# Audio tower on one core: W2 loaded and split in quarters, slot indices in one step on VectorE, waits and tables moved on ScalarE, new call orders in opening and ending

## The reference, cut to what matters

```python
# 1. tokens are merged: an MLP gives each token a length, the row is warped to 375 tokens
h = gelu(x @ W1 + b1)                       # 128 -> 512
h = gelu(h @ W2 + b2)                       # 512 -> 512
lens = sigmoid((h @ W3 + b3)[..., 0])
lens = lens / sum(lens) * 375
cs = cumsum(lens); h = warp(x, cs)          # piecewise linear weights, a matmul
# 2. linear attention with 8 memory keys, 8 heads of 64, residual
xn = rmsnorm(layernorm(h)); q, k, v = split(xn @ w_qkv)
context = softmax_over_tokens(k) @ v
h = h + rmsnorm((softmax(q) @ context) @ w_out + b_out)
# 3. switch layer, 16 experts, capacity 225 over all 8 * 375 tokens
xf = layernorm(h); probs = softmax(xf @ switch_w.T + switch_b)
routes = argmax(probs); pos = running count of the route; keep = pos < capacity
y = expert_w[routes] @ xf + expert_b[routes]
out = h + where(keep, y, xf) * max(probs)
```

## Time and profile before

| | us |
|---|---|
| median of 3 runs (lowest, highest) | 397.02 (396.35, 398.41) |
| profiled execution: its time | 397.55 |
| profiled execution: span | 395.8 |
| PE busy | 374.6 (95% of the span) |
| DVE busy | 331.1 (84%) |
| ACT busy | 227.5 (57%) |
| POOL busy | 142.0 (36%) |

### The profile page before, as it was taken

One profiled execution on the slowest core, in us unless ns is written; L12 is line 12 of the kernel. 1 busy time (PEld: TensorE's weight loads), 2 busy tenths in 40 slices (PEclk: granted clock), 3 DMA queues, 4 the chain that ended last, 5 costly groups with the idle time before them and its releaser, 6 DMA issues. The chain is left out here.

```text
span 395.8 us, 7949 instructions
## 1 busy us (share of the span) xinstructions
PE 374.6 (95%) x2706; PEld 326.0 (82%) x2706; DVE 331.1 (84%) x897; ACT 227.5 (57%) x432; POOL 142.0 (36%) x191
## 2 busy tenths in 40 slices
PE   7889989999999999999999999999999989999992
PEld 7667868898888889888888888888888778998892
DVE  3587759969897998889898989798998974988896
ACT  4633448915992499339943895279637743683200
POOL 6101110122168215831484038413840611106880
PEclk9999999999999999999999999999999999999998
DMA  7796002100200030002000200100000052241135
GB/s 220 192 228 235 2 1 55 30 2 3 84 2 20 3 84 2 21 1 84 2 18 5 84 2 11 58 1 1 17 7 0 9 144 69 70 131 31 40 83 127
DMA packets 16358, 21.58 MB, mean 55 GB/s; under 512 B 4882, under 2 KB 11880, under 8 KB 15886
## 3 DMA queue, kind: packets, MB, share of 16 engines
q1 hardware_dynamic: 12350, 18.30, 16.6%
q0 software_dynamic: 2880, 2.35, 2.5%
q10 hardware_dynamic: 1088, 0.42, 0.4%
HBM read 14.40 MB, written 6.62 MB: 53 GB/s over the span
## 5 line engine op out<-in xcount | busy, mean ns | idle before, releaser
L1081 PE MATMUL psB<-W2h,h1l 128*125 128x512 f32 x192 | 77.9, 406 | 2.0 <-DVE h2b L1623 1.3
L1082 PE MATMUL psB<-W2l,h1h 128*125 128x512 f32 x192 | 75.6, 394 | 0.0
L1083 PE MATMUL psB<-W2h,h1h 128*125 128x512 f32 x192 | 75.6, 394 | 0.0
L681 ACT ACTIVATE h2b<-h2b 125x512 f32<-125x512 f32 x48 | 30.1, 628 | 32.9 <-DVE h2b L1623 32.5
L1081 PEld LDWEIGHTS psB<-W2h,h1l 128*125 128x125 f32 x192 | 35.6, 185 | 9.9 <-issue 1.8
L1083 PEld LDWEIGHTS psB<-W2h,h1h 128*125 128x125 f32 x192 | 35.6, 185 | 8.9
L1082 PEld LDWEIGHTS psB<-W2l,h1h 128*125 128x125 f32 x192 | 35.7, 186 | 7.2
L670 ACT ACTIVATE h<-psA,b1c 128x376 f32<-128x376 f32 x64 | 35.4, 579 | 8.4 <-PE psA L1052 8.1
L1623 DVE TENSOR_TENSOR h2b<-psB,b2r 125x512 f32<-125x512 f32 x48 | 32.8, 686 | 8.0 <-PE psB L1083 7.8
L596 POOL DMA_INDIRECT slot_x<-xf,idx_s x18 | 32.5, 1807 | 7.8 <-issue 7.8
L1630 DVE CUSTOM_DVE_ANT_0 h2b<-h2b,W3r 125x512 f32<-125x512 f32 x48 | 32.9, 691 | 1.7 <-ACT h2b L681 1.4
(11 more groups left out here) (266 smaller groups left out, 967.8 us busy)
## 6 DMA issues: line engine op xcount, KB each, us to landing
xTf<-in_x_t SPq DMA_DIRECT2D x16, 187.5 KB, 2.6
xt<-in_x SPq DMA_DIRECT2D x8, 336.0 KB
slot_x<-eb_parts SPq DMA_DIRECT2D x2, 960.0 KB, 13.5
basef<-in_L_tok_W SPq DMA_DIRECT2D x1, 1024.0 KB, 6.9
ewT<-in_expert_t SPq DMA_DIRECT2D x1, 1024.0 KB, 9.3
ewf<-slot_x SPq DMA_DIRECT2D x2, 480.0 KB, 6.1
h2b<-slot_x SPq DMA_DIRECT2D x2, 480.0 KB, 8.5
slot_y<-h SPq DMA_DIRECT2D x4, 240.0 KB, 2.5
```

Of the source, the lines that this page charges most:

```text
L681: nc.scalar.activation(slot, slot, ACT.Gelu).then_inc(c_g2.sem, 1)
L1081: mm(ps, lo, W2h[:, k, :], start=k == 0, stop=False)
L1082: mm(ps, hi, W2l[:, k, :], start=False, stop=False)
L1083: last = mm(ps, hi, W2h[:, k, :], start=False, stop=k == HK - 1)
```

## The change

- **W2 in four parts.** SyncE loads W2 in four DMAs with a semaphore each. VectorE casts and subtracts each quarter as it comes, and makes `h1l` of row 0, first half, in two halves of its own (`h1_upper_first` on ScalarE gives the upper parts). TensorE's first two `layer2` calls are cut in two (`layer2_first`), so that the first two quarters can be used before the last two. Layer 1 of row 0 uses six banks instead of two, and starts with the product that needs no `W1l`. Two of the 14 warm-up matmuls go.
- **VectorE's setup** is cut into `scale_weights` (after `minus_z(0)`) and `split_weights` (after `warp_weights(0)`).
- **Slot indices in one step.** `place_in_expert` on VectorE computes index = 16 * position - rank in one call and the index for the gather in a second; GpSimd's nine calls and the `tok` and `place` tiles go. The scratch in DRAM is larger, so that tokens over the capacity have rows of their own by position. `keep` comes after the indices.
- **Waits.** `own_sigmoid` names its wait for z first. `root_table` moves from just ahead of `own_root2` to behind `route_exp(PRIOR - 1)`, ahead of `take_tokens(0)`.
- **Orders.** All engines' lists in `opening` and `ending` are rewritten; the steps' lists are the same. The gathers go 1, 5, 0, 4, 3, 2, the rows are finished in the order of before.

```diff
-            sp.dma_start(W2f, W2.rearrange("(k p) n -> p k n", p=128)).then_inc(s_w2, 16)
+            for k in range(HK):
+                sp.dma_start(W2f[:, k, :], W2[k * 128:(k + 1) * 128]).then_inc(s_w2[k], 16)
...
-                after(pool, c_pp, b, 2)
-                after(pool, c_rm, b, 1)
-                if prev is not None:
-                    after(pool, c_sct, prev, 48)
-                    after(pool, c_idx, prev, 9)
-                after(pool, c_keep, b, 1)
-                pool.tensor_scalar(place[:, 0], pos[:], float(E), None, ALU.mult).then_inc(c_idx.sem, 1)
                 after(pool, c_idx, b, 1)
-                pool.tensor_tensor(place[:, 1], place[:, 0], rm[:], ALU.subtract).then_inc(c_idx.sem, 1)
-                after(pool, c_idx, b, 2)
-                pool.tensor_tensor(place[:, 2], place[:, 1], tok[:], ALU.subtract).then_inc(c_idx.sem, 1)
-                after(pool, c_idx, b, 3)
-                pool.tensor_tensor(place[:, 3], place[:, 2], keep[:], ALU.mult).then_inc(c_idx.sem, 1)
-                after(pool, c_idx, b, 4)
-                pool.tensor_tensor(place[:, 4], place[:, 3], tok[:], ALU.add).then_inc(c_idx.sem, 1)
-                after(pool, c_idx, b, 5)
-                pool.tensor_copy(idx_s[:], place[:, 4]).then_inc(c_idx.sem, 1)
-
-                pool.tensor_scalar(place[:, 2], place[:, 4], float(SLOTS - 1), None, ALU.min).then_inc(c_idx.sem, 1)
-                pool.tensor_scalar(tok[:], tok[:], float(G), None, ALU.add).then_inc(c_idx.sem, 1)
-                after(pool, c_idx, b, 8)
-                pool.tensor_copy(idx_g[:, bass.ds(b * GJ, GJ)], place[:, 2]).then_inc(c_idx.sem, 1)
                 for j in range(GJ):
                     pool.indirect_dma_start(out=slot_x, out_offset=bass.IndirectOffsetOnAxis(ap=idx_s[:, j:j + 1], axis=0),
                                             in_=xf[:, j, :], in_offset=None,
-                                            bounds_check=SLOTS + N - 1, oob_is_err=True).then_inc(c_sct.sem, 16)
+                                            bounds_check=N * E - 1, oob_is_err=True).then_inc(c_sct.sem, 16)
...
-                fetch(0, 0, GJ)
                 fetch(1, 0, 1)
                 fetch(1, 1, GJ)
+                fetch(5, 0, GJ)
+                fetch(0, 0, GJ)
+                fetch(4, 0, GJ)
+                fetch(3, 0, GJ)
                 fetch(2, 0, GJ)
-                fetch(3, 0, GJ)
-                fetch(4, 0, GJ)
-                fetch(5, 0, GJ)
...
             def own_sigmoid(b, prev):
 
+                after(act, c_z, b, TJ)
                 act.wait_ge(s_prep, N_PREP)
                 after(act, c_s, prev, 2)
-                after(act, c_z, b, TJ)
                 nc.scalar.activation(sg[:, 1], z[:], ACT.Exp, bias=b3n[:, 0:1], scale=-1.0).then_inc(c_sig.sem, 1)
...
+                route_exp(PRIOR - 1, PRIOR - 2)
+                root_table()
                 take_tokens(0)
                 take_tokens(1)
+                xn_hi(LAST, PRIOR)
+                take_outputs(0)
+                take_tokens(2)
+                take_tokens(3)
+                take_outputs(1)
+                take_outputs(2)
                 memory_keys(LAST, 0)
-                xn_hi(LAST, PRIOR)
-                take_tokens(2)
-                take_outputs(0)
...
+            def layer2_first(j, ks):
+
+                _, cols = half_cols(j)
+                for k in ks:
+                    pe.wait_ge(s_w2l, k + 1)
+                    if k < 2:
+                        pe.wait_ge(s_h1l, 1)
+                    else:
+                        after(pe, c_h1l, 0, 1)
+                    hi, lo = h1h[:, k, 0, cols], h1l[:, k, 0, cols]
+                    ps = psB[j][0:TP, :]
+                    mm(ps, lo, W2h[:, k, :], start=k == 0, stop=False)
+                    mm(ps, hi, W2l[:, k, :], start=False, stop=False)
+                    last = mm(ps, hi, W2h[:, k, :], start=False, stop=k == HK - 1)
+                if HK - 1 in ks:
+                    last.then_inc(c_l2.sem, 1)
 
...
+                layer2_first(1, (0, 1))
+                layer2_first(0, (0, 1))
+                layer2_first(0, (2, 3))
+                layer2_first(1, (2, 3))
                 layer1(1, 0, 0, 0)
-                layer2(0, None, 1)
                 layer1(1, 0, 0, 1)
+                layer2(0, None, 2)
                 layer1(1, 0, 0, 2)
-                layer2(0, None, 2)
                 setup()
                 layer1(1, 0, 0, 3)
...
+                positions(PRIOR, None)
+                values(LAST, PRIOR, 0)
                 expert_tokens(7)
-                expert_products(5)
-                values(LAST, PRIOR, 0)
+                values(LAST, PRIOR, 1)
+                values(LAST, PRIOR, 2)
+                k_transposed(LAST, PRIOR, 0)
+                k_transposed(LAST, PRIOR, 1)
+                chosen_on_rows(PRIOR)
+                k_transposed(LAST, PRIOR, 2)
                 expert_products(6)
                 expert_products(7)
-                values(LAST, PRIOR, 1)
-                k_transposed(LAST, PRIOR, 0)
-                k_transposed(LAST, PRIOR, 1)
-                positions(PRIOR, None)
-                k_transposed(LAST, PRIOR, 2)
-                values(LAST, PRIOR, 2)
                 q_transposed(LAST, PRIOR, 0)
                 q_transposed(LAST, PRIOR, 1)
                 context(LAST, PRIOR)
-                chosen_on_rows(PRIOR)
+                dense_bias(PRIOR)
                 fold(LAST, PRIOR, None)
                 q_transposed(LAST, PRIOR, 2)
+                dense(PRIOR, 0)
...
                 bias2(LAST, PRIOR, 4)
-                query_sum(PRIOR, PRIOR - 1)
                 bias2(LAST, PRIOR, 5)
+                key_max(PRIOR, PRIOR - 1, 3)
                 dot3(LAST, PRIOR, 4)
                 dot3(LAST, PRIOR, 5)
-                key_max(PRIOR, PRIOR - 1, 3)
+                place_in_expert(PRIOR - 1, PRIOR - 2)
                 scan(LAST, PRIOR)
-                query_norm(PRIOR, PRIOR - 1)
                 lengths(LAST, PRIOR)
                 warp_weights(LAST, PRIOR)
-                probability(PRIOR - 1, PRIOR - 2)
+                query_sum(PRIOR, PRIOR - 1)
...
+                own_tokens(LAST, 15)
+                finish_row(0)
                 finish_row(1)
-                own_tokens(LAST, 15)
                 finish_row(2)
-                keep_base(LAST, PRIOR)
                 finish_row(LAST)
                 finish_row(3)
...
+                if not ends(b):
+                    if prev is not None:
+                        after(dve, c_sct, prev, 48)
+                    vec.scalar_tensor_tensor(idx_s[:], pos[:], float(E), rm[:], ALU.mult, ALU.subtract).then_inc(c_idx.sem, 1)
+                    after(dve, c_idx, b, 1)
+                    vec.tensor_scalar(idx_g[:, bass.ds(b * GJ, GJ)], idx_s[:], float(SLOTS - 1), None, ALU.min).then_inc(c_idx.sem, 1)
...
+            for pair in range(2):
+                for k in (2 * pair, 2 * pair + 1):
+                    dve.wait_ge(s_w2[k], 16)
+                    vec.tensor_copy(W2h[:, k, :], W2f[:, k, :]).then_inc(s_w2h, 1)
+                    dve.wait_ge(s_w2h, k + 1)
+                    vec.tensor_tensor(W2l[:, k, :], W2f[:, k, :], W2h[:, k, :], ALU.subtract).then_inc(s_w2l, 1)
+                ks = slice(2 * pair, 2 * pair + 2)
+                if pair == 0:
+                    dve.wait_ge(s_h1h, 1)
+                else:
+                    after(dve, c_h1h, 0, 1)
```

353 lines of the change are left out of this document (175 added, 178 removed).

## The result

| | before | after | after, second timing |
|---|---|---|---|
| median us (lowest, highest) | 397.36 (396.35, 398.41) | 412.14 (409.30, 414.25) | 410.18 (407.57, 413.31) |
| against before | | 1.038 [1.035, 1.041] | 1.030 [1.027, 1.034] |
| profiled execution: span | 395.8 | 409.6 | 411.6 |

What follows compares the result with a forecast made beforehand. TensorE was taken to bound the loop, VectorE's chain the end, with the gathers close behind. Profiled 397.55 - 0.5 (tail) + 3.6 (later first gather, opening's 2.3 included) gave 400.65, or 400.1 against the median; range 394.8 to 403.0 us.

Steps and rivals of the forecast that it cites:

- Opening: Start up to the loop: W2 in quarters and new orders end the opening 2.3 us earlier, bounds 1.3 and 3.5.
- Indices: Slot indices: nine GpSimd calls per row go, two VectorE calls of 0.2 us come, hidden in the loop: 0.
- The 2.4: Slot indices in the loop: cost of VectorE's added calls, 6 x 0.4 us, if VectorE were the bound.
- Ending up to the experts: Ending: scatters 4.9 us later make TensorE wait for the slots, so expert_tokens(0) is 1.7 late.
- Experts, products 6 and 7 behind other calls: Experts' stage on TensorE: calls ahead of products 6 and 7 cost 3.7 us, k_transposed(LAST)'s wait for ScalarE 0.4.
- take_outputs(7) to the first gather: VectorE after product 7: take_outputs(7) queues behind other calls, ending about 359.1; the first gather follows 4.8 us later.
- Tail: First gather to end: same gather pace, five rows finished after the last gather, 392.3 against 392.8 before: 0.5 us gained.
- this order has no slack: Gathers with row 2 last: a later first gather counts in full, 3.6 us with the opening's gain included.
- Root table: ScalarE in the ending: the moved Sqrt adds two table loads of 1.28 us; taken as 0, at most 1.3.
- A: Rival, late by little: faster scatters, no key_exp wait, take_outputs(7) at once, opening 3.0; 397.6 us, chance 0.22.
- B: Rival, faster: gathers not the limit, VectorE's chain decides; 394.2 to 395.1 us, down to 392; chance 0.18.
- C: Rival: ScalarE becomes the bound in the experts' stage by the added table load, 1.3 more, 401.4 us; chance 0.12.

Runs made afterwards that it cites:

- pool_order: Changed kernel with one GpSimd swap in the opening: differences of row 1 ahead of norm1 of row 0, as in the kernel before; 406.87 us.
- wait_old: Changed kernel with one thing undone: own_sigmoid waits for z last again, the early root_table stays; 406.45 us.
- fillers: Changed kernel with 15 more idle-work matmuls on TensorE ahead of expert_tokens(0), results unused; 407.02 us.
- tables_old: Changed kernel with the old activation table handling: root_table straight ahead of own_root2, own_sigmoid waiting for z last; 406.32 us.
- open_fill: Changed kernel with idle-work matmuls in the opening, 10 ahead of xn_transposed(0) and 5 ahead of values(0); 406.12 us.
- attend_first: Changed kernel with two TensorE calls swapped: attend of row 6 ahead of expert_tokens(0); 406.40 us.

## Why the prediction was wrong

The sign was right, and so were most of the places where time would be won and lost. The step that failed is that work of TensorE was priced at the full clock behind every new wait, in the opening and again in `attend(PRIOR)`; in the opening a collision of VectorE and GpSimd was booked as a gain besides. The bounds covered neither.

- **Opening, -2.3, measured +3.1 in the profiled execution.** The first two `layer2` were done at 16.25, with the layer-1 product behind them at 16.95 (forecast 16.4), and TensorE stood from 20.76 to 22.83 for the small loads (20.4 to 23.8). The step that failed is "Followed call by call with the trace's durations": the durations were those of the full clock. The wait of 2.07 is dearer than itself. Kernels with this opening whose wait was 1.72 to 1.86 kept the clock and reached the context at 71.5 to 72.2; those with 2.03 to 2.59 came at 73.8 to 75.2. Counted from the loads it is 49.2 to 49.3 us against 50.6 to 51.8, so the low clock alone costs 1.3 to 2.6 (pool_order, with another wait mended, is left out). Also "`norm1` no longer waits behind `differences(1)`" was booked as a gain; it made the two collide, 1.1 us and a low clock of 2.5 more.
- **Indices, 0, measured 1.0 to 1.3.** The step took VectorE as hidden everywhere because TensorE bounds the loop. In the loop this nearly held (0.4 to 0.6 in five steps), in the ending it did not. The 2.4 that it named had no part in the sum and was no rival.
- **Ending up to the experts, +1.7, measured +4.6.** Right: 0.8 for own_sigmoid (0.9), the wait for the slots, and that it takes the place of all gains. The gains themselves were not there: TensorE asked for the slots 0.9 later than before, counted from the context, and not 1.4 earlier; the wait hides it. The size failed at the slots: the first scatter was 4.9 late by forecast and 6.3 by the trace, as the new order made z's last dot 1.6 later; the three scatters took 5.4 (forecast 4.4 to 6.0); and the loads came 2.9 and not 1.8 behind them, as in wait_old they did. `warp_weights` beside the scatters was in the sum as a bound, but with a price for the scatters alone and none for what follows.
- **Experts, products 6 and 7 behind other calls: 4.1 forecast, 2.8 to 3.5 measured.** Missing was the half clock in `attend(PRIOR)`, 2.5 to 2.9 (fillers).
- **take_outputs(7) to the first gather: +0.6, measured +0.5. Tail: -0.5, measured -0.1**, with the wait of 5.50 ahead of `finish_row(2)` (forecast some 4). The claim that this order has no slack held; what it costs by itself is 0.5 to 1.2 us.
- **Root table: 0 taken, 0 measured** (wait_old, tables_old).

The forecast said +3.1 of span; 5.4 are missing in the opening, 2.9 on the way to the experts, 2.1 in their stage and 0.3 in small terms. Rivals A and B fell with the opening (B also asks for a first gather before 356; it came at 371.83), C with tables_old and wait_old. The Trainium skill (SBUF — State Buffer, "SBUF: two separate sides") calls the port pair of VectorE and GpSimd an exclusive lock, and says that while VectorE runs an instruction in a two-port mode GpSimd cannot write the descriptors of its DMAs. The traces agree that one waits for the other, at 0.34 us that became 1.55, and at a scatter of 1.25 that became 2.23; in which mode VectorE ran no trace shows. The forecast used the lock for the three scatters only, and not for `norm1` beside `differences(1)`. On the clock, the Trainium skill (TensorE: Matmul & The Clock Gate, "Part 1: The HAM clock gate (the "warmup" mystery)") says that it follows how busy TensorE has been; open_fill and fillers agree, with 1.00 where it had been 0.52 and 0.51. I had read no wait of before with that in mind, because no row there shows a fall.

**Open.** Why the small loads land at 22.3 in one execution and 26.3 in another was not tried. That z's last dot is late because `attend(PRIOR - 1)` moved is argued from the order of the calls; its share of the way to the experts was not separated.

## What to carry to other kernels

Where a reorder makes the bounding matrix engine wait at a new place, price the wait and, behind it, the same work at half the clock; check it against the neighbour executions, and if work is at hand put it into the gap (attend_first), otherwise idle matmuls. An engine that arrives early at a wait for a DMA has gained nothing, and its earlier calls may fall on the very calls that the DMA depends on: look at VectorE's long calls beside GpSimd's DMAs before moving either. Split a rewritten order at the points where old and new lists hold the same calls; the halves can then be run as hybrids, and a table of distances between fixed events compares them better than medians do.

## What was new about the hardware

- The granted clock was lower after each of nine waits for the small loads of 2.03 to 5.54 us, and after none of five of 1.72 to 1.86; it stayed low for some 3.4 to 6.8 us. It was lower too after a wait of 2.3 us with one of 1.16 close behind, and not after 1.22 and 1.16. At half the clock 24 matmuls took 5.34 us in place of 2.79 to 2.89.
- A VectorE call of 0.34 us took 1.55 beside a GpSimd call, and an indirect DMA on GpSimd 2.23 in place of 1.25 beside a VectorE call of 1.33 (eleven kernels); the load that waits for that DMA then started another 1.0 to 1.6 later in ten of them, and in one it did not. A gather's instruction took 2.31 in place of 1.28 beside VectorE's `finish_row` calls.
- The same eleven loads, issued alike, let TensorE go on at 22.3 to 26.3 us.
